# Two attention layers and a recurrent network on one core: channels laid out by place in the head, and one load issued earlier

## The reference, cut to what matters

```python
def layer0(x, mask, Wq, Wk, Wv, b):            # 16 heads of 16 channels
    Q, K, V = (heads(einsum('oc,bct->bto', W, x)) for W in (Wq, Wk, Wv))
    att = einsum('bhqd,bhkd->bhqk', Q, K) / sqrt(16) + b[0]
    att = softmax(att * m + (1 - m) * -1e30)    # m: mask over the keys
    return einsum('bhqk,bhkd->bhqd', att, V)    # back to (b, channels, t)

def layer1(x, mask, Wq, Wo):                    # 8 heads of 32 channels
    q = heads(x^T @ Wq.T)                       # queries = keys = values
    att = softmax((scores(q, q) / sqrt(32) * m_keys + (1 - m_keys) * NEG) * m_rows)
    return (att @ q) @ Wo.T
x = x + layer0(...);  x = x + layer1(...)
x = x + gru(x, ...)                             # 256 steps, state 512
x = x + layer3(x, ...)                          # pooled blocks, projection, layer norm
```

## Time and profile before

| | |
|---|---|
| median of three runs | 2045.66 us (2039.86 to 2045.85) |
| the profiled execution | 2037.87 us, of which 2036.1 us are the span |
| TensorE busy | 1840.3 us, 90% |
| VectorE busy | 1146.1 us, 56% |
| ScalarE busy | 795.9 us, 39% |
| GpSimd busy | 390.8 us, 19% |
| granted TensorE clock, mean | 0.969 |
| moved by DMA | 127.64 MB, mean 63 GB/s |

### The profile page before, as it was taken

How to read it: one execution, slowest core, us unless ns; L and a number is a source line. 1 busy time by engine, 2 the same in 40 slices (tenths; PEclk the granted TensorE clock), 3 DMA queues, 4 the chain that set the end, 5 groups by cost and what they waited for, 6 DMA issues and landing times. The chain is left out here.

```text
span 2036.1 us, 85468 instructions
## 1 busy us (share of the span) xinstructions
PE 1840.3 (90%) x37678; PEld 1258.0 (62%) x37678; DVE 1146.1 (56%) x3363; ACT 795.9 (39%) x2195; POOL 390.8 (19%) x862
## 2 busy tenths in 40 slices
PE   4959999999999999987899999999999999999974
PEld 2323444444444444443798888888888888888761
DVE  3746666666757575733355555555555555555567
ACT  0536565555556465643222222222222222222224
POOL 0120212112111212110121222211222212222113
PEclk7889999999999999997999999999999999999995
DMA  4645161525334252222200000000000000000002
GB/s 130 218 110 151 55 174 52 162 66 152 88 113 127 84 144 71 65 70 77 111 13 13 12 12 12 5 13 12 12 12 10 6 13 12 13 12 9 7 3 83
DMA packets 64241, 127.64 MB, mean 63 GB/s; under 512 B 14265, under 2 KB 20921, under 8 KB 60276
## 3 DMA queue, kind: packets, MB, share of 16 engines
q1 hardware_dynamic: 60796, 121.34, 20.3%
q0 software_dynamic: 3072, 0.82, 0.2%
HBM read 77.56 MB, written 37.85 MB: 57 GB/s over the span
## 5 line engine op out<-in xcount | busy, mean ns | idle before, releaser
L410 DVE TENSOR_REDUCE mx<-MX 128x1 f32<-128x512 f32 x768 | 486.8, 684 | 214.3 <-PE MX L530 213.9
L953 PE MATMUL gate<-whh,state 128*8 128x128 f32 x16384 | 497.8, 273 | 68.7 <-DVE state L869 68.0
L953 PEld LDWEIGHTS gate<-whh,state 128*8 128x8 f32 x16384 | 423.4, 91 | 138.3 <-DVE state L869 135.6
L466 ACT ACTIVATE pr<-ST 128x512 f32<-128x512 f32 x768 | 411.9, 600 | 173.6 <-PE ST L550 173.2
L953 PE MATMUL pg<-whh,state 128*8 128x128 f32 x8192 | 272.2, 273 | 0.0
L530 PE MATMUL MX<-K,Q 51*128 51x512 f32 (+1 forms) x768 | 244.6, 465 | 28.0 <-DMA Q<-d_rows 23.0
L901 ACT ACTIVATE rg<-pre 128x32 f32<-128x32 f32 x256 | 58.8, 230 | 535.9 <-DVE pre L849 535.9
L847 DVE STREAM_TRANSPOSE trn<-gate 128x128 f32<-128x128 f32 x256 | 81.1, 317 | 328.0 <-PE gate L953 328.0
L550 PE MATMUL ST<-Q,K 53*128 53x512 f32 (+1 forms) x768 | 242.1, 484 | 13.0 <-ACT pr L466 12.0
L550 PEld LDWEIGHTS ST<-Q,K 53*128 53x128 f32 (+1 forms) x768 | 99.1, 186 | 212.3 <-ACT pr L466 120.6
L953 PEld LDWEIGHTS pg<-whh,state 128*8 128x8 f32 x8192 | 225.1, 90 | 0.4 <-issue 0.4
(11 more groups left out here) (185 smaller groups left out, 1869.5 us busy)
## 6 DMA issues: line engine op xcount, KB each, us to landing
d_q<-hi_q SPq DMA_DIRECT2D x32, 256.0 KB
d_q<-lo_q SPq DMA_DIRECT2D x32, 256.0 KB
d_k<-hi_k SPq DMA_DIRECT2D x32, 256.0 KB
d_k<-lo_k SPq DMA_DIRECT2D x32, 256.0 KB
K<-d_k SPq DMA_DIRECT2D x64, 128.0 KB
Q<-d_q SPq DMA_DIRECT2D x64, 128.0 KB
K<-d_k SPq DMA_DIRECT2D x16, 512.0 KB
Q<-d_q SPq DMA_DIRECT2D x16, 512.0 KB
```

Source lines behind the costliest of these rows:

```text
L410: dve.reduce_max(mx[:, u, col:col + 1], bank[:, :], AX.X).then_inc(mx_red, 1)
L466: act.activation(pr[:, kc % 2, i], ST[n % 3][:, :], ACT.Exp, scale=SCALE[UNITS[w][0]]).then_inc(exped, 1)
L953: last = pe.matmul(bank[32 * j:32 * j + B, lo:hi], held[q][:, c, :], whh[:, c, o + lo:o + hi], start=first, stop=done)
```

## The change

Three things.

1. The output channels of the query and key projections are laid out by their place in the head: a half of a projection has its 128 partitions ordered (channel in the head, head) instead of (head, channel). The host orders the weights' rows so (`by_place`); `pieces` writes DRAM with the channel outermost, 16 or 32 rows instead of 8 or 4, and the layout in DRAM stays the same; `ident_r`, which turns layer 1's keys into values, gets its columns in the order that puts the heads back.
2. `load_in(it + 2)` is issued inside `second_layer(it, 0)`, after the four pieces and ahead of the stack, instead of behind it.
3. At the start x is issued first, then two weights, the mask, b0 and the third weight, and each of layer 0's weights has a semaphore of its own, which TensorE waits for at the projection or values product that reads it.

```diff
--- before.py
+++ after.py
@@ -82,7 +82,8 @@
         AV = pb("AV", [P, T])
         DN = pb("DN", [P, T])
 
-        w0_in, weights, const, masks_in, masks_out, xT_in = (sem(n) for n in ("w0_in", "weights", "const", "masks_in", "masks_out", "xT_in"))
+        w0_in = [sem(f"w0_in{i}") for i in range(3)]
+        weights, const, masks_in, masks_out, xT_in = (sem(n) for n in ("weights", "const", "masks_in", "masks_out", "xT_in"))
         mx_mm, mx_red, mxT_mm, nm_row, nm_split = (sem(n) for n in ("mx_mm", "mx_red", "mxT_mm", "nm_row", "nm_split"))
         st_mm, exped, av_mm, raw_ev, rawd_ev = (sem(n) for n in ("st_mm", "exped", "av_mm", "raw_ev", "rawd_ev"))
         den_mm, fin_mm, rden, yn = (sem(n) for n in ("den_mm", "fin_mm", "rden", "yn"))
@@ -227,11 +228,12 @@
 
         @block.sync
         def _(sp):
+            sp.dma_start(xin[:], x[:, :, 0, :]).then_inc(xin_in, 16)
+            sp.dma_start(w0[:, 0], wq0).then_inc(w0_in[0], 16)
+            sp.dma_start(w0[:, 1], wk0).then_inc(w0_in[1], 16)
             sp.dma_start(m8[:], mask).then_inc(masks_in, 16)
-            sp.dma_start(xin[:], x[:, :, 0, :]).then_inc(xin_in, 16)
             sp.dma_start(b8[:], b0.rearrange("(a n) -> a n", a=1).to_broadcast([B, 1])).then_inc(masks_in, 16)
-            for i, d in enumerate((wq0, wk0, wv0)):
-                sp.dma_start(w0[:, i], d).then_inc(w0_in, 16)
+            sp.dma_start(w0[:, 2], wv0).then_inc(w0_in[2], 16)
 
             def load_in(b):
                 if not there(b):
@@ -267,7 +269,8 @@
                 else:
                     wait(sp, lo_ev, "proj", (s, m), b)
                 for j, half in enumerate((hi, lo)):
-                    to = d_piece[s][j].rearrange("d (m h) t -> m h d t", m=2)[m]
+
+                    to = d_piece[s][j].rearrange("d (m h) t -> m d h t", m=2)[m]
                     sp.dma_start(to, half[s][:, m].bitcast(fp32)).then_inc(piece_out[s, m], 16)
 
             def stack(b, w):
@@ -311,6 +314,8 @@
             def second_layer(b, m):
                 for side in ("k1", "q1"):
                     pieces(b, side, m)
+                if m == 0:
+                    load_in(b + 2)
                 for w in units_of(1, m):
                     stack(b, w)
 
@@ -325,8 +330,8 @@
                     first_layer(it + 1)
                 if there(it):
                     second_layer(it, 0)
-                load_in(it + 2)
                 if not there(it):
+                    load_in(it + 2)
                     sp.dma_start(xT[:], xt_in).then_inc(xT_in, 16)
                     preload(sp)
                 if there(it):
@@ -343,7 +348,8 @@
             pool.memset(va[:], 1.0).then_inc(const, 1)
             pool.wait_ge(weights, 48)
             pool.tensor_copy(sel[:], ident[:, 0:97:32]).then_inc(const, 1)
-            pool.tensor_copy(ident_r[:], ident[:]).then_inc(const, 1)
+
+            pool.tensor_copy(ident_r[:].rearrange("p (h d) -> p h d", d=DH[1]), ident[:].rearrange("p (d h) -> p h d", d=DH[1])).then_inc(const, 1)
 
             def split_row(b, bank, u):
 
@@ -590,6 +596,8 @@
                     wait(pe, x1_sum, ("back", 0), (0, 1), b)
                 else:
                     pe.wait_ge(xin_in, 16 * (b + 1))
+                    if b == 0:
+                        pe.wait_ge(w0_in[0 if s == "q0" else 1], 16)
                 walk.clear()
                 for k in range(2):
                     last = pe.matmul(bank[:, :], w_[:, k, m * P:(m + 1) * P], src[:, k, :], start=k == 0, stop=k == 1)
@@ -598,6 +606,8 @@
             def values(b, bank, L, m):
                 if L == 1:
                     wait(pe, lo_ev, "proj", ("k1", 1), b)
+                elif b == 0:
+                    pe.wait_ge(w0_in[2], 16)
                 walk.clear()
                 for h in range(2):
                     if L == 0:
@@ -627,7 +637,6 @@
                         last = pe.matmul(bank[:, h * CH:(h + 1) * CH], ctxs[:, k, tok(2 * m + h)], w1[:, 1, k, :], start=k == 0, stop=k == 1)
                 last.then_inc(out_mm, 1)
 
-            pe.wait_ge(w0_in, 48)
             walk = Walk(pe)
             walk.run({"max": max_, "maxT": max_t, "score": score, "av": av, "den": den, "finish": finish, "proj": proj,
                       "values": values, "back": back, "out": out_})
@@ -1344,11 +1353,13 @@
     nc = _bacc.Bacc("TRN2", target_bir_lowering=False, num_devices=1)
     v = {k: _np.asarray(a) for k, a in inputs.items()}
     wt = lambda a: a.T.reshape(2, 128, 256).transpose(1, 0, 2)
+
+    by_place = lambda a, h: wt(a.reshape(2, h, 128 // h, 256).swapaxes(1, 2).reshape(256, 256))
     perm = lambda a: a.reshape(a.shape[:-1] + (4, 4, 32)).swapaxes(-3, -2).reshape(a.shape)
     ins = dict(xt=perm(v['x']).reshape(8, 256, 4, 128).transpose(3, 2, 1, 0),
                x=perm(v['x']).reshape(8, 2, 128, 512).transpose(2, 1, 0, 3), mask=perm(v['cond_2048']),
-               wq0=wt(v['L0_cond_Wq']), wk0=wt(v['L0_cond_Wk']), wv0=wt(v['L0_cond_Wv']), b0=v['L0_cond_b'],
-               wq1=wt(v['L1_cond_Wq']), wo1=wt(v['L1_cond_Wo']), **gru_inputs(v, _np))
+               wq0=by_place(v['L0_cond_Wq'], 8), wk0=by_place(v['L0_cond_Wk'], 8), wv0=wt(v['L0_cond_Wv']), b0=v['L0_cond_b'],
+               wq1=by_place(v['L1_cond_Wq'], 4), wo1=wt(v['L1_cond_Wo']), **gru_inputs(v, _np))
     arrays, d = {}, {}
     for name, a in ins.items():
         a = _np.ascontiguousarray(a)
```

## The result

The changed kernel takes 2017.81 us (median of four, 2016.02 to 2020.56), the one before 2044.39 us in the same comparison (2039.86 to 2045.85): a ratio of 0.9875, interval 0.9855 to 0.9895, or 26.6 us less. The forecast was 2013 us, in 2004 to 2028, faster.

What follows compares the result with a forecast made beforehand. The prediction took TensorE's waits for DMAs, at three places in attention, as what counts. Its terms sum to 29.0 us, giving 2008.9 us from the profiled execution or 2016.7 from the median; it said 2013, range 2004 to 2028.

Steps and rivals of the forecast that it cites:

- What bounds the kernel, and why the pieces are slow: Attention: TensorE's waits for DMAs count; pieces use four or eight engines, would use sixteen and land in 3.1 us.
- Rival (a): Pieces stay on four and eight engines, the layout having no effect: gain 9.1 us, 2029 to 2037 us; chance 0.05.
- The start: Up to TensorE's first maxima: pieces 3.9 us sooner less 0.9 us of delay, gain 3.0 us (-0.8 to 4.9).
- the mask's delay: At the start, mask and b0 stand behind xin and two weights, so VectorE is released at 6.3 us, 0.9 late.
- The gap: TensorE's xin wait at 136 us shrinks to 2.2 us: gain 15.3 us, plus 1.6 from the clock not falling.
- The short xin waits: TensorE's three short waits for xin, before 1000 us, go too: gain 1.1 us (0 to 1.1).
- Steady batches: The moved load_in waits for the next batch's values, leaving little of the pieces' gain: no loss, gain 0.
- The end: Last batch, 920 to 928 us: the whole stack wait of 8.0 us goes; low clock behind it 0 to 0.8, taken as 0.
- The sum: All places: 3.0 + 15.3 + 1.6 + 1.1 + 8.0 = 29.0 us, bounds 20.3 to 32.4.
- a sign of being wrong: A recurrent stretch, behind attention, of another length than before, which would be no work of the diff.
- Rival (c): Slower: rows of maxima land late behind full engines and a score waits in every unit; some 2052 us, chance 0.03.
- rival (b): A new wait between 140 and 180 us takes back half of 16.9 us: 2017 to 2025 us, chance 0.09.

Runs made afterwards that it cites:

- e3: The changed kernel with the start's order undone: mask, x, b0, then the three weights on one semaphore; 2016.24 us, ratio 0.9884.
- e7: The changed kernel with mask and b0 issued first, then x and the weights, and ScalarE's table loaded ahead; 2013.87 us, ratio 0.9845.
- e5: The kernel before, unchanged, run for a second trace; 2046.03 us in its one execution.
- e1: The kernel before with the new layout of query and key channels alone, start order and load place as before; 2027.14 us, ratio 0.9931.
- e2: The kernel before with only load_in moved ahead of the stack, pieces still on four and eight engines; 2034.88 us, ratio 0.9972.
- e6: The kernel before with the new layout for layer 1's keys and queries alone, load and start as before; 2032.22 us, ratio 0.9944.
- e4: The changed kernel, unchanged, run for a second trace; 2017.82 us, ratio 0.9890.
- e8: e7 with idle products in TensorE's short waits at the end of layer 1's last two batches; 2007.61 us, ratio 0.9820.
- e9: The kernel of e8 with 90 idle products ahead of TensorE's wait for the first stack; 2014.41 us, ratio 0.9859.

## Why the prediction was right

**What bounds the kernel, and why the pieces are slow**: right. Shares of 0.26 and 0.52 became 1.0; from the issue of the last of four pieces to that of the stack it is now 2.4 to 3.5 us at the two places where TensorE waits, and 3.1 was worked out for the landing. (Over the whole trace the `lo` pieces, the later of each pair, land 4.5 to 4.7 us after their issue in the median.) Rival (a) is out. By the rule of the Trainium skill (DMA: Bandwidth & Descriptors, why a DMA increments its semaphore by 16) 16 and 32 rows use all sixteen engines; the trace agrees, with shares of 1.03 and 1.04.

**The start**: forecast 3.0 us, measured 1.9, and 1.8 to 2.4 between the four traces that start as before (35.37 to 35.90) and the two of the changed kernel. With the products laid side by side, the lead over the first trace of before is 3.1 us in the first and 2.4 us in the second trace of the changed kernel at 100 us; what adds the rest on the way is no term of the forecast and isn't shown. The pieces gave 3.5 of the 3.9, the mask's delay took 1.3 at VectorE and 1.5 at anyc instead of 0.9. The direction of that part, a loss and no gain, was right, and e3 and e7 show it from both sides. The Trainium skill's rule that an engine takes its ring in order (same page, Queues, rings and completion order) agrees with them: VectorE is released at 2.6, 5.4 and 6.7 us with only the mask, 0.5 and 1.0 MB ahead of b0. What was too small is the delay, 0.9 instead of 1.3 us: it had a shift of 0.5 us for xin's earlier issue taken off, and 5.39 + 1.4 (from 4.6 to 6.0) without that shift gives 6.8, near the measured 6.69.

**The gap**: forecast 15.3 + 1.6. TensorE's lead was 2.3 us just ahead of it and 20.0 us behind it, so it grew by 17.8 us, of which 16.2 are waiting and 1.6 the clock. (Just ahead of the gap the granted clock dips in the changed kernel, and the transposes at 120.4 us take 1.97 us instead of 1.09; the lead, 3.5 us at 120 us, shrinks there by 1.2. The forecast has no such term; e5 loses 1.4 us at the same place without the change.) xin landed in 4.1 us instead of 4.6. e1 and e2 show that each half of the change alone leaves about 9 us of this wait: the load must be ahead of the stack, and the pieces ahead of the load must be quick.

**The short xin waits**: forecast 1.1; the lead grew from 20.0 to 21.4 us by the last batch. Either part does it: they are gone in e1 and in e2, too. **Steady batches**: forecast 0, and e6 agrees.

**The end**: forecast 8.0 and up to 0.8 for the clock, and this is the term that was mis-sized. What it said of the pieces came true: stack 4 of batch 7 is issued at 870.11 and stack 5 at 882.38, 21.4 us later in the time base of before, so 891.5 where 892.2 was forecast and 903.8 where it was 904. The wait went, but against the first trace the lead grows only from 21.0 us (transposes at 903.52 and 882.54) to 22.3 at the end of attention, by 1.3 us; against e5 it grows from 22.8 to 27.7, by 4.9. The prediction's "The products behind it run at the low clock, but VectorE's maxima pace them" asked about the clock only right behind the wait. Two other places cost more. Ahead of the wait, the transposes (1.97 instead of 1.09 us) and the first group of output products run slow in the changed kernel. In e5 they do, too, but there the wait hides it: the output products are 2.0 us slower than in the first trace of before and the wait behind them 3.8 us shorter. In the changed kernel the same slowness lies bare. And behind the wait, the second group and its transposes are 2.3 us slower than in the first trace of before, as they are in e5 (2.5 us). So the term was read from a trace that had both groups at full clock and the longest wait; with e5 as the base the wait itself would have been 4.2 us.

**The sum**: 29.0 us forecast. By the medians 26.6 us were measured in the first comparison and 22.8 us in that of e4; to the end of attention it is 27.7 and 26.9 us between e5 and the two traces of the changed kernel, and 22.3 us between the first traces. The terms were worked out on the first trace of before, and against that trace only 17.3 us came. Of the two bases the median was the better one: the traced execution of before (2037.87) was nearly the quickest of all runs of that kernel (2037.84 to 2046.89). From the median the forecast was 2016.7, 1.1 us off, from the traced execution 2008.9, 8.9 us off. That the stated 2013 is within 5 us is in part luck: it lies between the two bases, and the shortfall at the end was masked in the medians by the runs of before being slower than its trace.

In the part behind attention the changed kernel's trace shows 5.0 us more, which the prediction named as a sign of being wrong; e5 has 2.8 of these without the change, and the code there is the same. In both, TensorE stands 5 us instead of 2 in the first products of that part, for nothing that the profile shows. But little of the loss is there: laid product by product beside the first trace of before, the changed kernel loses 0.4 us in the first 22 us of that part (a group of 128 records takes 3.70 us in it and 5.37 in the trace of before), 3.2 us in the next 100 us, at a granted clock of 1.00, and 1.4 us in the rest; e5 loses 1.0, 0.2 and 1.6 us. Rival (c) is out: the rows of the maxima land in 1.9 us, 5.6 at most. Of rival (b) nothing is seen: no new wait for a transfer comes behind the gap.

What stays open: why the clock falls in the first group of output products in eight traces of nine and not in the ninth; why the products behind attention take longer in most traces than in the first of before; and how the 6.3 us between e7 and e8 are made up.

## What to carry to other kernels

Read the DMA share while one kind of transfer moves alone: 0.26 of sixteen engines is four, and here it was the target's outermost dimension that had the size four. A chain of small transfers that ends in a computation goes ahead of large loads in the queue, even where TensorE's first product reads the large ones. A wait that is about to go may hide slow work ahead of it, so size its removal by the work that then lies bare, and take more than one trace of the kernel before a term rests on its clock.

## What the runs showed of the hardware

- The outermost size of a piece's target went with the DMA share while pieces moved alone: 4 rows 0.26 and 101 GB/s, 8 rows 0.52 and 181 GB/s, 16 rows 1.03 and 375 GB/s, 32 rows 1.04 and 404 GB/s, each with 128 partitions of source.
- A transfer queued behind others on only four engines lands with them: xin, itself spread, took about 10 us (e2) against 4.1 us with the same pieces on sixteen.
- Behind a row of idle waits of 0.7 to 1.3 us the 16 records of output products took 5.4 to 6.7 us in eight traces of nine, against 3.72 in the ninth; where the stretch was read (the changed kernel), the granted clock was 0.50. With idle products in these waits they took 3.72 us in three traces of three, at 1.00 (e8, 870 to 881 us).
- Keeping TensorE busy through the long wait ahead of the first maxima, which VectorE paces, gained nothing: the clock was down again within 8 us of the last idle product (e9, 0.57 from 40 to 44 us), and the way from the first maxima to the end of attention took 917.3 us against 916.8.
